# Weight preparation of a seven-product feed-forward kernel: from bf16 on single buffers to byte pairs and fp8 on double buffers

## The chip, the cores and the metric

The kernel runs on all 8 cores of one Trainium2 chip. Each core takes half of one of the 4 sequences and writes its own 4096 tokens of the output; nothing is exchanged between cores. The metric is the device time of the slowest core, in microseconds. Each core has a matrix engine (TensorE, in the rows PE, with its weight loads as PEld), a vector engine (DVE), a scalar engine (ACT), GpSimd (POOL) and a queue engine (SP). Each works through its own list of instructions in order. Transfers are issued from the queues of SP, ACT and POOL and are carried out by 16 DMA engines.

## The reference

```python
x = L0_attn_x                                  # (4, 8192, 1024) f32
xn = layernorm(x)
k, v, q = fft(xn @ Wk.T + bk), fft(xn @ Wv.T + bv), fft(xn @ Wq.T + bq)
queried = cumsum(k * v, axis=1) * conj(q)
attn = real(ifft(queried / (1e-9 + norm(queried)))) / sqrt(1024)
w(kb) = where(kb, +1.0, -1.0)                  # kb: booleans, one byte each
h = s0 * (concat([xn, -xn]) @ w(k0))           # k0 (2048, 4096)
h = s1 * (relu(h) * 2 @ w(k1))                 # k1 (4096, 4096)
h = s2 * (relu(h) * 2 @ w(k2))                 # k2 (4096, 1024)
out = x + attn + h
```

## The kernel before

A core has 4096 tokens, in 8 tiles of 512 (`t` = 0 to 7). The work has four stages.

1. Normalization of the extra half, a Gram matrix, and the fold of the three attention matrices with the Fourier matrix (0 to about 178 us).
2. The carry: the running sum over the tokens ahead of the core's own. PE and DVE alternate over nine steps (`carry_sums`, `products`); ACT takes its result out of PSUM (`evict(CH_CARRY, ...)`), and DVE scales it.
3. The projection loop, eight tiles. For each tile PE makes 24 chunks of 8 matmuls (`project(t, i)`, L684) and, after chunks 17 and 21, two inverse transforms each of the tile before (`inverse`, L739). ACT takes each chunk out of PSUM (`evict_proj`, recorded at L870), each inverse with two passes (`evict_inverse`, L970 and L973), and normalizes the next tile (`normalize`, L844 to L863). Four PSUM banks serve the chunks, so PE may be four chunks ahead of ACT. DVE takes six chunks at a time: `elementwise(t, mb)`, `mb` = 0 to 3 (L1206 to L1235), needs the eviction of chunk 6·mb+5. Once a tile it makes the `statistics` of the tile after the next (L1054 to L1066).
4. The feed-forward part, layers (0, t), (1, t), (2, t). Each matrix product is done with 7 instead of 8 block products ("P1" to "P7", L818 for layers 0 and 1, L796 for layer 2); ACT copies partial results (`snap`, L1007), DVE adds them. The weight operands are fp8 and stream from DRAM (`w0c`, `w1c`, `w2c`) into a ring.

The seven weight operands have to be made first, from boolean bytes. That is the **weight preparation**. It is cut into 48 units (8 for layer 0, 32 for layer 1, 8 for layer 2). A unit is four quarters of 128x1024, one byte per weight. Before, a unit goes like this:

- its bytes are loaded into `raw` (two buffers): by SP for the units of layer 0, two loads each (`load_first`, L461), otherwise by ACT's queue (L878);
- for layer 0 DVE first combines the two loads, in pairs of bytes (`ternary`, L1084);
- ACT turns all 4096 columns into bf16 +1/-1 (or +1/0/-1), with the sign of the layer's scale in it, in two activations of 3072 and 1024 columns (`prepare` of ACT, L896), into `wq`, of which there are two until tile 7 and one from there on;
- DVE makes the sums of quarters with four bf16 `tensor_sub` (`prepare` of DVE, L1093 to L1098): one into `wq` itself, three into `ws`, of which there is one;
- POOL stores four blocks from `wq` (L1383) and three from `ws` (L1385); both stores change bf16 to fp8 on the way.

ACT may not write a `wq` before its last store has landed, and DVE may not write `ws` before the last store of `ws` has landed (`s_ps`).

The order of all this is written out by hand. DVE has, for tile t of 1 to 7, with units u-5 to u-1 of the tile: elementwise 0, u-5, u-4, elementwise 1, u-3, u-2, elementwise 2, statistics, u-1, elementwise 3 (tile 7 has four units). ACT has u-5, u-4, u-3, u-2, u-1 behind chunks 5, 8, 11, 15 and 19. Seven units (`FIRST_UNITS`) fall in the carry stage and tile 0, and the last seven (`SPOTS`) between the evictions of layer (1, 0).

Of the kernel before, what the change touches and what calls it, by code (L numbers as in the profile page):

```python
# [12 lines left out]
BF16 = mybir.dt.bfloat16  # L13
# [13 lines left out]
NST = 8  # L27
# [122 lines left out]
PROD_AT = {"P1": 0, "P7": 1, "P2": 2, "P4": 3, "P3": 4, "P5": 5, "P6": 6}  # L150
# [14 lines left out]

UNITS = ([(0, mh, m) for mh in range(4) for m in range(2)]
# [3 lines left out]
HALF_UNIT = [u for u in range(len(UNITS)) for _ in range(2 if u < 8 else 1)]  # L170
# [5 lines left out]
FIRST_UNITS = 7  # L176
# [36 lines left out]
def build_nc():  # L213
# [40 lines left out]
    s_ps = sem("s_ps")  # L254
# [27 lines left out]
    s_pa = sem("s_pa")  # L282
    s_snap = sem("s_snap")
# [53 lines left out]
    def layout(part, *specs):  # L337

        made, pos = {}, 0
        with ExitStack() as stack:  # L340
            for at, name, shape, dt, size in specs:
# [29 lines left out]
                *[(40 + 2 * i, f"kv{i}", [128, D], BF16, 2) for i in range(2)],  # L371
                (48, "z1", [128, NMB * D], BF16, 8),
# [42 lines left out]
    xt = {p: ld["xt" + p] for p in ("P4", "P5", "P6", "P7")}  # L415
    xn_b, xa, part_b = ld["xn_b"], [ld[f"xa{i}"] for i in range(4)], [ld[f"part{i}"] for i in range(4)]

    wq, ws = [lc["wq0"], lc["wq1"]], lc["ws"]
    xsum, xsum_h = lb["xsum"], lb["xsum_h"]

    def own_block(t):

        return xn_t if t else lb["xn_t0"]

# [1077 lines left out]
```

## Time and profile before

| | us |
|---|---|
| median of 3 runs | 3181.21 (3179.56 to 3186.8) |
| the profiled execution, its own time | 3180.06 |
| its span, core 4 (the slowest) | 3178.3 |
| spans of the 8 cores | 3163.4 to 3178.3 |
| TensorE busy in the span | 2971.2 (93%) |
| DVE, ACT, POOL busy | 1235.5, 839.8, 216.8 |
| carry stage | 178 to 231 |
| projection loop, eight tiles | 231 to 784 |
| feed-forward part | 783 to 3178 |

A row of the timeline has the start, the duration, the engine, the line in the kernel, the operation, output <- input, and how many instructions are merged in it; what stands in brackets is the idle time of the engine ahead of it and what ended it. A row of the waits has who waited for whom, the sum in us, how many times, and the longest. The span starts at 0, and all rows are of core 4.

### The profile page before, as it was taken

To read this page: it belongs to the slowest core of one execution; us is meant where nothing else is said; L and a number is where in the kernel's file an instruction comes from. 1 tells how busy PE (TensorE), PEld (TensorE's weight loads), DVE (VectorE), ACT (ScalarE), POOL (GpSimd) and SP (SyncE) were. 2 spreads that over 40 slices of the span, in tenths; PEclk is the share of its full clock that TensorE was granted. 3 is DMA by queue.
4 is the path that set the end of the run, shared out by engine and by line. 5 is a ranking of instruction groups with operands and counts; after the bars stand their busy time and mean duration, and the time that the engine had idled before them with its cause. 6 is when DMAs were issued, how large, how long until landed. Compare 5 with 4: busy or idle time off the path is not lost.

```text
span 3178.3 us, 57905 instructions; the slowest of 8 cores (3163.4 to 3178.3 us)
## 1 busy us (share of the span) xinstructions
PE 2971.2 (93%) x22472; PEld 2191.4 (69%) x22472; DVE 1235.5 (39%) x2503; ACT 839.8 (26%) x1172; POOL 216.8 (7%) x268
## 2 busy tenths in 40 slices
PE   6787777878999999999999999999999999999997
PEld 3333233334788868868886888688778868886884
DVE  6476566657422522152134124321611251243113
ACT  6345666665331200120111002011200110121000
POOL 7100111111000000000000000000000000000000
PEclk8898898888999999999999999999999999999999
DMA  8675889886687464456446644644564456446543
GB/s 279 186 186 126 178 200 191 198 181 147 187 216 215 157 224 151 136 176 220 152 133 195 203 153 145 234 153 140 169 223 151 132 180 220 150 134 225 161 151 113
DMA packets 235339, 561.68 MB, mean 177 GB/s; under 512 B 54336, under 2 KB 99392, under 8 KB 231488
## 3 DMA queue, kind: packets, MB, share of 16 engines
q1 hardware_dynamic: 166256, 423.21, 43.2%
q0 software_dynamic: 60032, 102.78, 13.8%
q10 hardware_dynamic: 8784, 31.99, 3.4%
q8 instruction: 186, 3.05, 0.4%
q14 instruction: 81, 0.66, 0.1%
HBM read 463.52 MB, written 85.98 MB: 173 GB/s over the span
## 4 chain that ended last, share of the span: by engine, by line
PE 76%; DMA 9%; DVE 8%; issue 3%; SPq 1%; ACT 1%; DVEq 0%; ACTq 0%; POOL 0%; POOLq 0%
PE pd L818 61%; PE pd L796 12%; DMA w1c<-ws 6%; DVE kv L1218 1%; DVE stats L1054 1%; DMA xring<-x_extra 1%; PE pd L684 1%; SPq L481 1%; DMA w0c<-ws 1%; DVE wq L1095 1%; DVE ws L1093 1%; DVE ws L1096 1%; DMA wtmp<-Wmat 1%; PE pd L600 0%; DVE ws L1098 0%
## 5 line engine op out<-in xcount | busy, mean ns | idle before, releaser
L818 PE MATMUL pd<-r0P,ring 128*128 128x256 f16 x14336 | 1568.7, 273 | 7.2 <-ACT snap L1007 7.2
L818 PEld LDWEIGHTS pd<-r0P,ring 128*128 128x128 fp8e4 x14336 | 1403.8, 98 | 172.8 <-issue 8.0
L1007 ACT ACTIVATE snap<-pd 128x512 f32<-128x512 f32 x432 | 257.4, 597 | 1732.6 <-PE pd L818 1456.9
L1337 DVE SCALAR_TENSOR_TENSOR r1P<-pd,snap 128x512 f16<-128x512 f32 x128 | 88.5, 692 | 904.0 <-ACT snap L1007 621.1
L796 PE MATMUL pd<-ring,r1P 128*128 128x512 fp8e4 x1792 | 389.8, 380 | 5.1 <-DVE r1P L1354 5.1
L796 PEld LDWEIGHTS pd<-ring,r1P 128*128 128x128 f16 x1792 | 175.7, 98 | 216.3 <-issue 7.5
L1337 DVE SCALAR_TENSOR_TENSOR b<-pd,snap 128x512 f16<-128x512 f32 x128 | 88.6, 692 | 407.3 <-PE pd L818 407.3
L896 ACT ACTIVATE wq<-raw,s_scales 128x3072 bf16<-128x3072 uint8 x96 | 195.8, 2089 | 192.9 <-DMA w1c<-wq 74.6
L818 PE MATMUL pd<-xtP,ring 128*128 128x256 f16 x2048 | 234.4, 272 | 4.7 <-issue 0.9
L684 PE MATMUL pd<-xn_f,Ak 128*128 128x512 f16 x512 | 147.3, 450 | 83.1 <-ACT proj L870 83.0
L818 PEld LDWEIGHTS pd<-xtP,ring 128*128 128x128 fp8e4 x2048 | 195.9, 98 | 38.0 <-issue 13.4
L818 PE MATMUL pd<-xn_b,ring 128*128 128x256 f16 x1536 | 177.4, 275 | 5.8 <-ACT squares L973 5.8
L684 PEld LDWEIGHTS pd<-xn_f,Ak 128*128 128x128 bf16 x512 | 55.6, 111 | 168.6 <-issue 137.0
L818 PEld LDWEIGHTS pd<-xn_b,ring 128*128 128x128 fp8e4 x1536 | 151.7, 99 | 25.5 <-issue 6.3
L684 PE MATMUL pd<-xn_f,Av 128*128 128x512 f16 x512 | 124.0, 398 | 16.9 <-ACT proj L870 16.9
L684 PE MATMUL pd<-xn_f,Aq 128*128 128x512 f16 x512 | 125.4, 402 | 13.8 <-ACT proj L870 13.8
L870 ACT ACTIVATE proj<-pd,bcol 128x512 bf16<-128x512 f32 x192 | 119.9, 691 | 29.2 <-PE pd L684 29.0
L1337 DVE SCALAR_TENSOR_TENSOR r0P<-pd,snap 128x512 f16<-128x512 f32 x128 | 85.5, 687 | 88.8 <-ACT snap L1007 88.4
L684 PEld LDWEIGHTS pd<-xn_f,Av 128*128 128x128 bf16 x512 | 51.7, 102 | 87.3 <-issue 43.5
L684 PEld LDWEIGHTS pd<-xn_f,Aq 128*128 128x128 bf16 x512 | 52.0, 102 | 82.4 <-issue 35.9
L577 PE MATMUL pd<-xn_x 128*128 128x512 f16 (+3 forms) x384 | 74.4, 361 | 29.9 <-ACT xn_x L863 29.9
L1093 DVE TENSOR_TENSOR ws<-wq 128x1024 bf16<-128x1024 bf16 x48 | 33.0, 689 | 162.7 <-DMA w1c<-ws 121.0
(147 smaller groups left out, 1795.4 us busy)
## 6 DMA issues: line engine op xcount, KB each, us to landing
ring<-w1c SPq DMA_DIRECT2D x448, 512.0 KB, 4.0
ring<-w0c SPq DMA_DIRECT2D x224, 256.0 KB, 2.7
ring<-w2c SPq DMA_DIRECT2D x112, 512.0 KB, 4.9
raw<-kraw ACTq DMA_DIRECT2D x39, 512.0 KB, 6.6
xring<-x_extra SPq DMA_DIRECT2D x32, 512.0 KB, 7.9
w1c<-wq POOLq DMA_DIRECT2D x32, 512.0 KB, 5.5
xa<-x_own POOLq DMA_DIRECT2D x32, 512.0 KB, 12.5
out<-xa POOLq DMA_DIRECT2D x32, 512.0 KB, 8.4
```

What stands on the lines that cost most here:

```text
L481: sync.dma_start(xn_f[t % 2][:, dk * TST:(dk + 1) * TST], xn_dram.ap()[t * TST:(t + 1) * TST, dk * 128:(dk + 1) * 128], transpose=True).th ...
L577: mm = te.matmul(pd[pair][:, at:at + hi - lo], xb[:, i * 128:(i + 1) * 128], xb[:, lo:hi], start=(tb == 0 and at % 512 == 0), stop=(tb == ...
L684: mm = te.matmul(bank, sA[p][:, dk * D + cs.start: dk * D + cs.stop], xn_f[t % 2][:, dk * TST:(dk + 1) * TST], start=(dk == 0), stop=(dk = ...
L796: mm = te.matmul(bank, r1[prod_][:, kt * 256 + q * 128: kt * 256 + (q + 1) * 128], ring[n % RING][:, (kt % 8) * 512:(kt % 8 + 1) * 512], s ...
L818: mm = te.matmul(bank[:, mi * 256:(mi + 1) * 256], ring[n % RING][:, at:at + 128], rhs, start=(opens and kt == 0 and mi == 0), stop=(close ...
L870: sc.activation(dst, src, AF.Identity if kw else AF.Copy, **kw).then_inc(s_ev, 1)
L896: op = sc.activation(wq[BUF[u]][:, lo:hi], raw_t[h % 2][:, lo:hi], AF.Identity, scale=s_scales[:, at:at + 1], bias=s_scales[:, to:to + 1])
L1007: sc.activation(snap[i][q][:], banks[0][q], AF.Copy, scale=scale).then_inc(s_snap, 1)
L1054: own(v.bn_stats(stats[b][:, (2 * j + h) * 6:(2 * j + h + 1) * 6], xring[x_slot(c)][:, h * 512:(h + 1) * 512]))
L1093: own(v.tensor_sub(s1, a21, a22))
L1095: v.tensor_sub(a21, a11, a21).then_inc(s_pq, 1)
L1337: v.scalar_tensor_tensor(dst[q], banks[bk][q], scale, snap[si][q][:], op0=OP.mult, op1=OP.add).then_inc(done, 1)
```

## The change

It replaces the number format and the buffers of the weight preparation and reorders it.

- **Layers 1 and 2, per unit.** DVE writes three quarters as finished fp8 bytes straight from `raw`, two bytes at a time as one uint16 (two `tensor_scalar`, 1024 and 512 elements, into `w8q`). It makes the four sums, again in pairs of bytes (512 elements each), with three `scalar_tensor_tensor` and one `tensor_sub`, into `sums` (uint8). ACT converts `sums` to fp8 `w8s`, in two activations of 3072 and 1024 columns.
- **Layer 0, per unit.** The combination of the two loads goes to its own buffer `tern`. ACT converts three quarters of `tern` to fp8 (2048 and 1024 columns, `prepare_quarters`), and later the sums.
- **Stores** take fp8 as it is: three blocks from `w8q`, four from `w8s`. There are two of `raw`, `w8q`, `sums` and `w8s`, and one of `tern`.
- **Loads of `raw`** are all issued by POOL, in between its stores (`load_raw`).
- **Order.** DVE now comes ahead of ACT in each unit; before it was behind. The places on ACT are the same for tiles 1 to 7. DVE's places move ahead by one elementwise. Eight units are in the carry stage and tile 0, six in layer (1, 0).
- **Signs** of s0 and s1 are no longer in the weights but in the scale that ACT and DVE use when they take products out of PSUM (`layer_scale`).
- The sum "P5" of the normalized input overwrites its place in `xn_b`; the order of blocks in DRAM and of quarters in `kraw` changes.

```diff
-FIRST_UNITS = 7
+FIRST_UNITS = 8
...
-BUF = [u % 2 if u < OWN_UNITS[NST - 1][0] else 0 for u in range(len(UNITS))]
...
+                *[(108 + 4 * i, f"w8s{i}", [128, 4 * 1024], F8, 4) for i in range(2)],
+                (116, "tern", [128, 4 * 1024], U8, 4),
...
+                *[(192 + 4 * i, f"sums{i}", [128, 4 * 1024], U8, 4) for i in range(2)],
+                *[(200 + 3 * i, f"w8q{i}", [128, 3 * 1024], F8, 3) for i in range(2)])
...
+    def layer_scale(layer):
+
+        return (s_scales[:, 8:9], s_scales[:, 4:5], 1.0)[layer]
...
+        def convert(dst, src, scale, bias):
+
+            at = 10 + (-4, -3, -1, 1).index(bias)
+            return sc.activation(dst, src, AF.Identity, scale=scale, bias=s_scales[:, at:at + 1], saturate=False)
+
+        def prepare_quarters(u):
+
+            sc.wait_ge(s_tern, u + 1)
+            if u >= 2:
+                sc.wait_ge(s_po[u % 2], 16 * (u // 2))
+            convert(w8q[u % 2][:, 0:2048], tern[:, 0:2048], 1.0, -1)
+            convert(w8q[u % 2][:, 2048:3072], tern[:, 2048:3072], -1.0, 1).then_inc(s_pa0, 1)
+
         def prepare(u):
...
+            scale = 2.0 if UNITS[u][0] else 1.0
+            sc.wait_ge(s_pd, u + 1)
+            if u >= 2:
+                sc.wait_ge(s_ps[u % 2], 16 * (u // 2))
+            convert(w8s[u % 2][:, 0:3072], sums[u % 2][:, 0:3072], scale, -4)
+            convert(w8s[u % 2][:, 3072:4096], sums[u % 2][:, 3072:4096], scale, -3).then_inc(s_pa, 1)
...
-        for u in range(3):
+        for u in range(4):
+            prepare_quarters(u)
             prepare(u)
         evict(CH_CARRY, red[:], singles[CH_CARRY % 4][:, 0:12])
...
-            if i in (2, 8, 14, 20):
-                prepare(3 + i // 6)
+            if i % 6 == 1:
+                prepare_quarters(4 + i // 6)
+            if i % 6 == 4:
+                prepare(4 + i // 6)
...
+                v.scalar_tensor_tensor(tern[:].bitcast(U16), raw_t[0][:].bitcast(U16), 257.0,
+                                       raw_t[1][:].bitcast(U16), op0=OP.add, op1=OP.subtract).then_inc(s_tern, 1)
...
+                own(v.tensor_scalar(q[:, 0:1024], src[:, 0:1024], -128.0, float(0xB8B8), op0=OP.mult, op1=OP.add))
+                v.wait_ge(s_dve, nv)
+                v.tensor_scalar(q[:, 1024:1536], src[:, 1024:1536], 128.0, float(0x3838),
+                                op0=OP.mult, op1=OP.add).then_inc(s_pq, 1)
...
+            own(v.scalar_tensor_tensor(o1, a21, f * 0x0101, a22, op0=OP.add, op1=OP.add))
+            own(v.scalar_tensor_tensor(o7, a11, f * 0x0202, a21, op0=OP.add, op1=OP.subtract))
             v.wait_ge(s_dve, nv)
...
+            own(v.tensor_sub(o2, o1, a11))
             v.wait_ge(s_dve, nv)
-            v.tensor_sub(s4, a12, s2).then_inc(s_pd, 1)
+            v.scalar_tensor_tensor(o4, a12, f * 0x0303, o2, op0=OP.add, op1=OP.subtract).then_inc(s_pd, 1)
...
         for mb in range(NMB):
+            prepare(4 + mb)
             elementwise(0, mb)
-            prepare(3 + mb)
-            ternary(4 + mb)
         for t in range(1, NST):
             units = list(OWN_UNITS[t])
-            elementwise(t, 0)
             if t < NST - 1:
                 prepare(units[-5])
             prepare(units[-4])
+            elementwise(t, 0)
+            prepare(units[-3])
             elementwise(t, 1)
-            prepare(units[-3])
             prepare(units[-2])
...
+            g.dma_start(dst[:, 0:3], w8q[u % 2][:].rearrange("p (r k) -> p r k", r=3)).then_inc(s_po[u % 2], 16)
+            if layer and u + 2 < len(UNITS):
+                load_raw(u + 2)
+            g.wait_ge(s_pa, u + 1)
+            g.dma_start(dst[:, 3:7], w8s[u % 2][:].rearrange("p (r k) -> p r k", r=4)).then_inc(s_ps[u % 2], 16)
```

The three places where the order of instructions matters for what follows. First DVE in tile 1 to 5, from the statistics (L1054 before) to the start of elementwise 3 (`u<-proj`). Before:

```order
L1054 BN_STATS stats<-xring 128x6 x8
L1058 BN_AGGR mv<-stats 128x2 x4
L1064 TENSOR_SCALAR nmean<-mv 128x4
L1066 COPY var<-mv 128x4
L1093 TENSOR_TENSOR ws<-wq 128x1024
L1095 TENSOR_TENSOR wq<-wq 128x1024
L1096 TENSOR_TENSOR ws<-ws,wq 128x1024
L1098 TENSOR_TENSOR ws<-wq,ws 128x1024
L1206 TENSOR_TENSOR u<-proj 128x1024
```

The same place in the changed kernel:

```order
L1032 BN_STATS stats<-xring 128x6 x8
L1036 BN_AGGR mv<-stats 128x2 x4
L1042 TENSOR_SCALAR nmean<-mv 128x4
L1044 COPY var<-mv 128x4
L1075 TENSOR_SCALAR w8q<-raw 128x1024
L1077 TENSOR_SCALAR w8q<-raw 128x512
L1087 SCALAR_TENSOR_TENSOR sums<-raw 128x512
L1088 SCALAR_TENSOR_TENSOR sums<-raw 128x512
L1090 TENSOR_TENSOR sums<-sums,raw 128x512
L1092 SCALAR_TENSOR_TENSOR sums<-raw,sums 128x512
L1199 TENSOR_TENSOR u<-proj 128x1024
```

The unit stands at the same place, but its input is `raw` and no longer ACT's `wq`: here DVE waited for ACT before, and ACT waits for DVE now.

Second ACT at the end of the carry stage: the units between the normalization of tile 1 and the eviction of the carry (`red<-pd`), and the first of tile 0. Before:

```order
L896 ACTIVATE wq<-raw,s_scales 128x3072
L896 ACTIVATE wq<-raw,s_scales 128x1024
L896 ACTIVATE wq<-raw,s_scales 128x3072
L896 ACTIVATE wq<-raw,s_scales 128x1024
L870 ACTIVATE red<-pd 128x12
L870 ACTIVATE proj<-pd,bcol 128x512 x3
L896 ACTIVATE wq<-raw,s_scales 128x3072
L896 ACTIVATE wq<-raw,s_scales 128x1024
L870 ACTIVATE proj<-pd,bcol 128x512 x6
```

In the changed kernel:

```order
L856 ACTIVATE w8q<-tern,s_scales 128x2048
L856 ACTIVATE w8q<-tern,s_scales 128x1024
L856 ACTIVATE w8s<-sums,s_scales 128x3072
L856 ACTIVATE w8s<-sums,s_scales 128x1024
L851 ACTIVATE red<-pd 128x12
L851 ACTIVATE proj<-pd,bcol 128x512 x2
L856 ACTIVATE w8q<-tern,s_scales 128x2048
L856 ACTIVATE w8q<-tern,s_scales 128x1024
L851 ACTIVATE proj<-pd,bcol 128x512 x3
L856 ACTIVATE w8s<-sums,s_scales 128x3072
L856 ACTIVATE w8s<-sums,s_scales 128x1024
L851 ACTIVATE proj<-pd,bcol 128x512 x3
```

A unit of layer 0 now has two places on ACT instead of one, and the eviction of the carry stands behind four units instead of three.

Third POOL in the projection loop. Before, and then in the changed kernel:

```order
L1383 DMA w1c<-wq 128x4x1024
L1385 DMA w1c<-ws 128x3x1024
L1383 DMA w1c<-wq 128x4x1024
L1385 DMA w1c<-ws 128x3x1024
L1390 DMA partial_dram<-eo 128x1024 x2
```

```order
L1396 DMA w1c<-w8q 128x3x1024
L1382 DMA raw<-kraw 128x4096
L1400 DMA w1c<-w8s 128x4x1024
L1396 DMA w1c<-w8q 128x3x1024
L1382 DMA raw<-kraw 128x4096
L1400 DMA w1c<-w8s 128x4x1024
L1405 DMA partial_dram<-eo 128x1024 x2
```

The load of a unit's bytes has moved in between the two stores of the unit two ahead of it.

## Rows read from the trace of the kernel before

**Rows 1.** The page: busy time, and chain that ended last by line.

```profile
PE 2971.2 (93%) x22472; PEld 2191.4 (69%) x22472; DVE 1235.5 (39%) x2503; ACT 839.8 (26%) x1172; POOL 216.8 (7%) x268
...
PE pd L818 61%; PE pd L796 12%; DMA w1c<-ws 6%; DVE kv L1218 1%; DVE stats L1054 1%; DMA xring<-x_extra 1%; PE pd L684 1%; SPq L481 1%; DMA w0c<-ws 1%; DVE wq L1095 1%; DVE ws L1093 1%; DVE ws L1096 1%; DMA wtmp<-Wmat 1%; PE pd L600 0%; DVE ws L1098 0%
```

**Rows 2.** Waits, 300 to 784 us (DVE and ACT).

```profile
DVE ws L1093 <- DMA w1c<-ws: 121.0, 18, 11.5
DVE ws L1093 <- DMA w0c<-ws: 17.7, 2, 11.8
...
ACT wq L896 <- DMA w1c<-wq: 74.6, 16, 9.9
```

**Rows 3.** Timeline of ACT: evictions that end tile 0 and tile 7.

```profile
298.61 2.39 ACT L870 ACTIVATE proj<-pd,bcol 128x512 bf16<-128x512 f32 x4
...
782.93 1.29 ACT L870 ACTIVATE proj<-pd,bcol 128x512 bf16<-128x512 f32 x2
```

**Rows 4.** Timeline of DVE, 516 to 540 us: statistics, one unit, two elementwise.

```profile
516.01 4.84 DVE L1054 BATCH_NORM_STATS2 stats<-xring 128x6 f32<-128x512 f32 x8
...
521.99 0.69 DVE L1093 TENSOR_TENSOR ws<-wq 128x1024 bf16<-128x1024 bf16 x1
...
524.79 0.69 DVE L1206 TENSOR_TENSOR u<-proj 128x1024 bf16<-128x1024 bf16 x1
...
531.51 0.68 DVE L1206 TENSOR_TENSOR u<-proj 128x1024 bf16<-128x1024 bf16 x1
...
538.92 0.41 DVE L1235 COPY z<-u 1x1024 bf16<-1x1024 bf16 x1
```

**Rows 5.** Timeline of ACT, 572 to 584 us: one unit, evictions, two inverses.

```profile
572.75 4.08 ACT L896 ACTIVATE wq<-raw,s_scales 128x3072 bf16<-128x3072 uint8 x2 [4.09 <-DMA w1c<-wq]
576.74 1.24 ACT L870 ACTIVATE proj<-pd,bcol 128x512 bf16<-128x512 f32 x2
577.88 1.00 ACT L970 CAST eo<-pd 128x1024 bf16<-128x1024 f32 x1
...
581.67 2.45 ACT L870 ACTIVATE proj<-pd,bcol 128x512 bf16<-128x512 f32 x4
```

**Rows 6.** Groups by line and shape, 0 to 1000 us: busy, mean ns.

```profile
L896 ACT ACTIVATE wq<-raw,s_scales 128x3072 bf16<-128x3072 uint8 x48 | 141.6, 2949 | 192.9 <-DMA w1c<-wq 74.6 <-DVE raw L1084 45.1 <-DMA w2c<-wq 42.3
...
L896 ACT ACTIVATE wq<-raw,s_scales 128x1024 bf16<-128x1024 uint8 x48 | 59.0, 1230 | 0.0
...
L1084 DVE SCALAR_TENSOR_TENSOR raw<-raw 128x2048 uint16<-128x2048 uint16 x8 | 18.3, 2288 | 3.3 <-DMA raw<-kraw 3.3
...
L1231 DVE TENSOR_TENSOR z<-y 128x512 bf16<-128x512 bf16 x32 | 13.4, 420 | 0.0
...
L1341 DVE TENSOR_SCALAR r0P<-r0P 128x512 f16<-128x512 f16 x16 | 3.9, 285 | 0.0
...
L1235 DVE COPY z<-u 1x1024 bf16<-1x1024 bf16 x8 | 3.3, 415 | 0.8
```

**Rows 7.** The instructions that touch the tile `raw`, 500 to 585 us: its loads.

```profile
DMA to landing us min/median/max: 5.2/7.1/13.6
```

**Rows 8.** Timeline of ACT, 231 to 259 us: eviction of the carry, a unit of tile 0.

```profile
231.20 0.18 ACT L870 ACTIVATE red<-pd 128x12 f32<-128x12 f32 x1 [9.21 <-PE pd L700]
...
258.66 4.08 ACT L896 ACTIVATE wq<-raw,s_scales 128x3072 bf16<-128x3072 uint8 x2 [7.39 <-DVE raw L1084]
```

**Rows 9.** Timeline of DVE, 227 to 230 us: the ninth and last `products`.

```profile
227.81 1.21 DVE L1172 TENSOR_TENSOR prod<-brow_k,pd 1x1024 bf16<-1x1024 bf16 x1 [5.06 <-PE pd L718]
```

**Rows 10.** Waits of PE, 784 to 3178 us.

```profile
PE pd L818 <- ACT snap L1007: 7.2, 1, 7.2
```

**Rows 11.** Timeline of PE: layer (1, 0) from 847 us, the start of (0, 1), and (1, 1).

```profile
847.22 84.03 PE L818 MATMUL pd<-r0P,ring 128*128 128x256 f16 x768
...
1052.35 3.66 PE L818 MATMUL pd<-xn_b,ring 128*128 128x256 f16 x32
...
1150.84 195.79 PE L818 MATMUL pd<-r0P,ring 128*128 128x256 f16 x1792
```

More of the change, by code:

```diff
@@ L253, in build_nc @@
     s_po = [sem(f"s_po{i}") for i in range(2)]
-    s_ps = sem("s_ps")
+    s_ps = [sem(f"s_ps{i}") for i in range(2)]
     s_xnw = sem("s_xnw")
@@ L414, in build_nc @@
     r1 = {p: ld["r1" + p] for p in ORDER}
-    xt = {p: ld["xt" + p] for p in ("P4", "P5", "P6", "P7")}
+    xt = {p: ld["xt" + p] for p in ("P4", "P6", "P7")}
     xn_b, xa, part_b = ld["xn_b"], [ld[f"xa{i}"] for i in range(4)], [ld[f"part{i}"] for i in range(4)]
-    wq, ws = [lc["wq0"], lc["wq1"]], lc["ws"]
+    tern, sums = lc["tern"], [lc["sums0"], lc["sums1"]]
+    w8q, w8s = [lc["w8q0"], lc["w8q1"]], [lc["w8s0"], lc["w8s1"]]
     xsum, xsum_h = lb["xsum"], lb["xsum_h"]
@@ L994, in _ @@
         for layer, t in LAYERS:
-            scale = C1 if layer == 1 else 1.0
+            scale = layer_scale(layer)
             if (layer, t) == (1, 0):
@@ L1007, in _ @@
                         sc.activation(snap[i][q][:], banks[0][q], AF.Copy, scale=scale).then_inc(s_snap, 1)
-                    for u in SPOTS.get((layer, t, pair, i), ()):
-                        prepare(u)
+                    if (layer, t, pair, i) in SPOTS:
+                        prepare(SPOTS[(layer, t, pair, i)])
                 if layer < 2:
@@ L1016, in _ @@
                                       scale=scale).then_inc(s_c21a, 1)
-                for u in SPOTS.get((layer, t, pair, 3), ()):
-                    prepare(u)
+                if (layer, t, pair, 3) in SPOTS:
+                    prepare(SPOTS[(layer, t, pair, 3)])
                 if (layer, t) == (0, 0):
@@ L1131, in _ @@
         v.wait_ge(s_dve, nv)
-        for dst, src, f in ((4, 7, 2.0), (5, 7, -1.0), (6, 7, -2.0), (9, 8, -1.0)):
-            own(v.tensor_scalar(s_scales[:, dst:dst + 1], s_scales[:, src:src + 1], f, None, op0=OP.mult))
+        own(v.tensor_scalar(s_scales[:, 4:5], s_scales[:, 7:8], C1, None, op0=OP.mult))
         own(v.scalar_tensor_tensor(s_scales[:, 0:1], s_scales[:, 0:1], 2048.0, s_scales[:, 8:9],
@@ L1155, in _ @@
         gram_done(v)
-        own(v.memset(ones_t[:], 1.0))
         own(v.memset(t16[:], TC * GSCALE))
@@ L1280, in _ @@
         for layer, t in LAYERS:
[L1281 removed]
+            scale = layer_scale(layer)
             if (layer, t) == (1, 0):
@@ L1341, in _ @@
                         own(v.tensor_scalar(dst[q], dst[q], 0.0, None, op0=OP.max))
-                    for u in SPOTS.get((layer, t, pair, i), ()):
-                        prepare(u)
+                    if (layer, t, pair, i) in SUM_SPOTS:
+                        prepare(SUM_SPOTS[(layer, t, pair, i)])
                 v.wait_ge(s_dve, nv)
@@ L1355, in _ @@
                                  b21[q]).then_inc(s_r0 if layer == 0 else s_r1, 1)
-                for u in SPOTS.get((layer, t, pair, 3), ()):
-                    prepare(u)
+                if (layer, t, pair, 3) in SUM_SPOTS:
+                    prepare(SUM_SPOTS[(layer, t, pair, 3)])
                 if layer == 1 and pair == 1 and t + 1 < NST:
@@ L1422, in _ @@
                 for i in range(4):
-                    for u in SPOTS.get((layer, t, pair, i), ()):
-                        store_unit(u)
+                    if (layer, t, pair, i) in SPOTS:
+                        store_unit(SPOTS[(layer, t, pair, i)])
             if layer == 0 and t + 1 < NST:
```

152 lines of the change are left out of this document (62 added, 90 removed).

## Prediction, made before the run

> **What bounds the kernel now.** I read the page first, then the chain that ended last, the waits of the engines, and last the timelines of DVE and ACT side by side. By the page PE is busy 93% of the span, and the chain goes through PE's feed-forward lines for 73% of it; the next line is a transfer, `w1c<-ws`, with 6% [rows 1]. So there are two regimes. In the feed-forward part PE is the bound, and nothing in the weight preparation can change that except where PE stands still: once, 7.2 us, for a `snap` of ACT [rows 10]. In layer (1, 0) PE needs 205.1 us (847.22 to 1052.35) for what it does in 195.6 us in layer (1, 1) (195.79, the last matmul overlapping the next): 9.5 us are lost there [rows 11].
>
> The other regime is the projection loop. From the end of tile 0 (298.61 and three evictions of 0.58, the fourth is tile 1's: 300.3) to the end of tile 7 (784.2) it takes 483.9 us for seven tiles, 69 us each [rows 3]. None of the engines is full in it; DVE waits 121.0 and 17.7 us for stores of `ws` to land, ACT 74.6 us for stores of `wq` [rows 2]. With one `ws` a unit can't begin before the store of the last has landed. The change removes just this. The question is what comes late next.
>
> **The cost of a unit after the change.** DVE's prices from rows: a two-source operation on 512 two-byte elements 0.42, the `scalar_tensor_tensor` on 2048 uint16 2.29, so one element per cycle, and 0.69 for 512 (2.29 less 1536 elements at 1.04 ns); one-source operations on two-byte elements in SBUF 0.285 for 512 and 0.415 for 1024 [rows 6]. Two instructions follow each other 0.08 us before the end of the first, or 0.1 us after it where the second waits for it: the old unit, four of 0.69, takes 2.80 so (521.99 to 524.79) [rows 4]. A new unit of layers 1 and 2 is then 0.52 + 0.20 + 0.61 + 0.79 + 0.52 + 0.61 = 3.25 us, and a unit of layer 0 is 2.39 + 2.53 = 4.9. No row has a one-source operation on uint16. Its bounds are the rows above (0.42 and 0.285) and one element per cycle, 1.21 for 1024 (here with an input in PSUM) [rows 9] and 0.69 for 512, which would make the unit 4.45. I take the lower one, since the rows of bf16 and f16 agree with each other and differ from uint16 in the type alone; the upper one is a rival. ACT's unit stays at 4.0 us (572.75 to 576.74) [rows 5], because the same 3072 and 1024 columns go through; fp8 out instead of bf16 has no row, and what speaks for the same price is that ACT's time goes by columns (1230 and 2949 ns for 1024 and 3072) [rows 6]. The quarters of layer 0 come to 2.09 + 1.23 less the overlap of 0.17, 3.15 us.
>
> The Trainium skill ("Vector Engine (DVE) Microarchitecture Reference", section 5.1) asks for two-byte types, and not for floats, before a one-source operation takes four elements per cycle, and does not list `scalar_tensor_tensor` among the operations that have a fast mode. By it the unit is 3.25; no run here shows it for uint16 yet.
>
> **The loop after the change, step by step.** Elementwise is 6.7 us (524.79 to 531.51), 7.75 with row 0 (531.51 to 539.25), statistics 6.0 (516.01 to 521.99) [rows 4], an eviction 0.58, two inverses 3.8 to 3.9 (577.88 to 581.67) [rows 5]. I begin at the last eviction of a tile, which frees elementwise 3:
>
> - DVE: elementwise 3 (6.7), two units (6.5), elementwise 0 (7.75), unit u-3 (3.25), elementwise 1 (6.7), unit u-2 (3.25): 34.15. In this stretch ACT is ahead of DVE except at u-3, where it catches up.
> - ACT at chunk 15 has been waiting for this unit: conversion 4.0, evictions 16 and 17, 1.2: 5.2.
> - DVE, which waited for chunk 17: elementwise 2 (6.7), statistics (6.0), unit u-1 (3.25): 15.95.
> - ACT at chunk 19 has been waiting for that: conversion 4.0, evictions 20 and 21, two inverses, evictions 22 and 23: 10.3.
>
> With four hand-offs of 0.1 that is 66.0 us. The wait for the store is gone, but DVE's unit now stands ahead of ACT's, and ACT's conversions of u-2 and u-1 stand ahead of the evictions that DVE needs. So DVE's idle time of 5.2 and 10.3 us a tile takes the place of the waits for `ws`. PE is hidden: while ACT waits it fills the four banks. The stores are hidden: each has over 14 us until its buffer is wanted, and the same buffer is two units away. Tile 6 has no statistics, 60.0. Tile 7 has one unit fewer too, 56.7; its sums of the input (four operations of 0.69) fit in the 5.2 us in which DVE waits. Tiles 1 to 7: 330 + 60.0 + 56.7 = 446.7, against 483.9: **37.2 us less**.
>
> **The carry stage and tile 0.** Here work is added. The eviction of the carry, at 231.2 now [rows 8], stands behind four units. DVE's last `products` end at 230.3 (227.81 and 2.5) [rows 9]; without the waits for `raw` (3.3 us in all [rows 6]) and with a first unit that is 2.6 us longer I put them at 228.5. Then `tern` (230.8), ACT's quarters (234.1), its sums (238.1), the eviction 238.4. Carry 1.2, statistics 6.0, `tern` 2.4: 248.0; quarters 3.15, three evictions, sums 4.0, one eviction: chunk 5 at 257.6. From there each six chunks take one elementwise, `tern` 2.4, quarters 3.2, four evictions 2.3, sums 4.0 and 0.2 of hand-offs: 19.8, 18.8, 18.8. Tile 0 ends at 315.0, against 300.3: **14.7 us more**. Now the distance of two units is 18.0 (258.66 to 276.64 in the timeline whose first row is in rows 8).
>
> **Layer (1, 0).** Six units instead of seven, each of DVE one step ahead of ACT's, and a store buffer that is two units old. ACT's conversion of 4.0 us stands behind a `snap` and ahead of the next, which PE wants only two products (14 us) later. I find no wait that would reach PE: **9.5 us less**, all of it. The signs in the evictions change an immediate into a scalar operand; costed at nothing, since DVE and ACT wait for PE there. The order of the sums of the input, one longer chain (0.8 us), lies behind layer 1's work of PE.
>
> **Sum.** 14.7 - 37.2 - 9.5 = -32.0. I take 1 off for hand-offs that I haven't seen and get -31: 3180.06 - 31 = 3149, and the median shown is 1.15 above that execution: **3150 us**.
>
> **Rivals.**
>
> *One element per cycle for the uint16 `tensor_scalar`* (the slower side). A unit is 1.2 us longer. All of DVE's units in tiles 1 to 7 are on the path above, 5 x 5 + 5 + 4 = 34: +41 us, so 3150 + 41 = 3191, slower by 0.3%. It decides from 0.9 us a unit on. For it: the uint16 operation that has a row runs so; against it: that one has two sources. 10%.
>
> *Loads of `raw` come late from POOL's queue.* The load of u-3 is issued when DVE is done with u-5, and is wanted after u-4 and elementwise 0, 3.25 + 7.75 = 11.0 us later. A load lands in 5.2 to 13.6 us now, median 7.1 [rows 7]. If all took 13.6 the tile would be 2.6 us longer, 7 x 2.6 = 18: 3168. The other loads have 20 us and more. Against it: stores read half the bytes in SBUF, so the queues are emptier. 8%. The Trainium skill ("SBUF — State Buffer", section "SBUF: two separate sides") has a rule that bears on it: while DVE runs an operation that uses both port pairs, GpSimd can't write descriptors, and it advises the ACT or SP queue. By that each load could be late by one such operation, 0.42 us, inside the slack of 3.9; so far no row here shows such a delay.
>
> *The waits go and nothing replaces them.* If ACT's conversions were not in DVE's way, DVE would lose its 15.5 us a tile, 7 x 15.5 = 108: 3042. For it: the engines are each busy under 50 us a tile. Against it: the lists are in order, and the evictions of chunks 16 and 20 stand behind conversions. 5%.
>
> *The stores stay the bound.* If fp8 stores landed no sooner than 13.8 us and the two buffers did not help, the projection loop would stay and tile 0 would cost its 14.7: 3181 + 14.7 - 9.5 = 3186. Against it is the distance of two units. 3%.
>
> **How the numbers follow.** The forecast has 74%, its own range 3150 +- 14 (2 us a tile); the rivals 10, 8, 5 and 3%. The range from 3130 to 3174 holds the forecast but for a few per cent, and the late loads, about 79%; I widen it to 3128 to 3176. A measurement of this kernel can tell about 0.2%, 6 us. Faster by more than that: forecast, late loads, no replacement, less a tail: 0.84. Within: 0.05. Slower: 0.11.
>
> **What would show it.** In the profile after: DVE's `w8q<-raw` at 0.42 and 0.285 us; no DVE wait for a store in the loop, but DVE waiting for ACT's `proj` twice a tile, about 5 and 10 us, and ACT's `w8s` waiting for DVE's `sums`, up to 11 us; tile 0 ending near 315 and tile 7 near 762; tiles of 66 us; PE without a gap in layer (1, 0). It is wrong if tiles take under 60 or over 70 us, if ACT's conversion is longer than 4.1 us, or if the first tile ends before 305.

## The result, and the profile after

The changed kernel takes **3149.4 us** (median of 20 executions). Against the kernel before on the same chip that is a ratio of **0.9909**, 95% interval 0.9886 to 0.9931, so 22 to 36 us less. In some executions one die or both ran at a lower granted clock and took up to 15% longer, with most of the kernels here; such executions (they lift the median of before to 3207 us) are left out of all that follows. The forecast was 3150 us, in a range from 3128 to 3176.

The profiled execution took 3149.38 us, and the span of its slowest core (core 5) is 3147.8. First come two lines of the page, to be read against [rows 1]: busy time, and the chain that ended last by line.

```profile
PE 2952.8 (94%) x22472; PEld 2187.8 (70%) x22472; DVE 1272.4 (40%) x2579; ACT 898.1 (29%) x1188; POOL 246.6 (8%) x324
...
PE pd L799 62%; PE pd L777 12%; PE pd L665 7%; DVE stats L1032 2%; ACT w8s L856 1%; ACT proj L851 1%; DMA xring<-x_extra 1%; PE pd L720 1%; DVE kv L1211 1%; DVE tern L1066 1%; SPq L472 1%; DMA wtmp<-Wmat 1%; PE pd L581 0%; PE pd L696 0%; DVE wsd L1052 0%
```

The store `w1c<-ws` with its 6% is gone from the chain. Next come the waits of DVE and ACT from 300 to 765 us (total, times, longest), to be read against [rows 2]:

```profile
DVE u L1199 <- ACT proj L851: 114.0, 15, 10.7
...
ACT w8s L856 <- DVE sums L1092: 121.6, 27, 11.7
```

No wait for a store is left in that stretch, and each engine waits for the other. The timeline of DVE for the second half of one tile (start, duration, in brackets the idle time before) shows where, beside the statistics at 491.72:

```profile
476.00 0.42 DVE L1075 TENSOR_SCALAR w8q<-raw 128x1024 uint16<-128x1024 uint16 x1
...
478.66 0.69 DVE L1092 SCALAR_TENSOR_TENSOR sums<-raw,sums 128x512 uint16<-128x512 uint16 x1
485.00 0.69 DVE L1199 TENSOR_TENSOR u<-proj 128x1024 bf16<-128x1024 bf16 x1 [5.64 <-ACT proj L851]
...
500.72 0.69 DVE L1092 SCALAR_TENSOR_TENSOR sums<-raw,sums 128x512 uint16<-128x512 uint16 x1
511.77 0.69 DVE L1199 TENSOR_TENSOR u<-proj 128x1024 bf16<-128x1024 bf16 x1 [10.36 <-ACT proj L851]
```

ACT's timeline beside it: the conversion that had waited for these sums runs first, and of the evictions behind it the two at 483.58 and the first two of the four at 510.30 are what DVE waits for.

```profile
479.78 3.90 ACT L856 ACTIVATE w8s<-sums,s_scales 128x3072 fp8e4<-128x3072 uint8 x2 [4.06 <-DVE sums L1092]
483.58 1.24 ACT L851 ACTIVATE proj<-pd,bcol 128x512 bf16<-128x512 f32 x2
...
501.56 3.89 ACT L856 ACTIVATE w8s<-sums,s_scales 128x3072 fp8e4<-128x3072 uint8 x2 [11.74 <-DVE sums L1092]
505.36 1.24 ACT L851 ACTIVATE proj<-pd,bcol 128x512 bf16<-128x512 f32 x2
...
510.30 2.46 ACT L851 ACTIVATE proj<-pd,bcol 128x512 bf16<-128x512 f32 x4
```

The same timeline has the eviction of the carry and those that end tile 0 and tile 7, to be read against [rows 3, 8]:

```profile
236.75 0.16 ACT L851 ACTIVATE red<-pd 128x12 f32<-128x12 f32 x1
...
311.45 1.26 ACT L851 ACTIVATE proj<-pd,bcol 128x512 bf16<-128x512 f32 x2
...
760.98 1.30 ACT L851 ACTIVATE proj<-pd,bcol 128x512 bf16<-128x512 f32 x2
```

Of the last pair at 311.45 the first ends tile 0, at 312.1; tile 7 ends at 762.3. Tiles 1 to 7 take 450.2 us instead of 483.8. In the feed-forward part PE's timeline shows layer (1, 0) without a gap, but PE's waits from 761 to 3147 us have 31 short waits for `snap`. Before, there was one wait for `snap`, in layer (1, 0) [rows 10]; that its 7.2 us equal the new sum is chance:

```profile
823.19 195.79 PE L799 MATMUL pd<-r0P,ring 128*128 128x256 f16 x1792
```

```profile
PE pd L799 <- ACT snap L985: 7.2, 31, 0.4
```

The groups by line and shape (busy, mean ns) are to be read against [rows 6]:

```profile
L985 ACT ACTIVATE snap<-pd,s_scales 128x512 f32<-128x512 f32 x384 | 263.5, 687 | 1463.8 <-PE pd L799 1462.3 <-DMA partial_dram<-eo 1.5
...
L856 ACT ACTIVATE w8s<-sums,s_scales 128x3072 fp8e4<-128x3072 uint8 x48 | 136.9, 2852 | 121.8 <-DVE sums L1092 121.8
L1331 DVE SCALAR_TENSOR_TENSOR r1P<-pd,s_scales,snap 128x512 f16<-128x512 f32 x128 | 96.1, 751 | 908.1 <-ACT snap L985 627.1 <-PE pd L799 281.0
...
L856 ACT ACTIVATE w8s<-sums,s_scales 128x1024 fp8e4<-128x1024 uint8 x48 | 54.5, 1135 | 0.0
...
L985 ACT ACTIVATE snap<-pd 128x512 f32<-128x512 f32 x48 | 28.7, 597 | 274.3 <-PE pd L777 274.3
...
L1075 DVE TENSOR_SCALAR w8q<-raw 128x1024 uint16<-128x1024 uint16 x40 | 16.7, 418 | 0.4 <-issue 0.4
...
L1077 DVE TENSOR_SCALAR w8q<-raw 128x512 uint16<-128x512 uint16 x40 | 11.8, 295 | 4.2
```

### The profile page after: what moved, and what is told of

The parts are those of the page before. It is cut to its first block, busy times and chain, and to the rows that moved or that the text cites. A ratio compares the mean times of both kernels' runs of the same rounds, so it can differ in the third digit from the quotient of the medians.

```text
span 3147.8 us, 58054 instructions; the slowest of 8 cores (3140.1 to 3147.8 us)
## 1 busy us (share of the span) xinstructions
PE 2952.8 (94%) x22472; PEld 2187.8 (70%) x22472; DVE 1272.4 (40%) x2579; ACT 898.1 (29%) x1188; POOL 246.6 (8%) x324
## 4 chain that ended last, share of the span: by engine, by line
PE 84%; DVE 6%; issue 4%; ACT 3%; DMA 2%; SPq 1%; ACTq 0%; DVEq 0%; POOLq 0%; POOL 0%
PE pd L799 62%; PE pd L777 12%; PE pd L665 7%; DVE stats L1032 2%; ACT w8s L856 1%; ACT proj L851 1%; DMA xring<-x_extra 1%; PE pd L720 1%; DVE kv L1211 1%; DVE tern L1066 1%; SPq L472 1%; DMA wtmp<-Wmat 1%; PE pd L581 0%; PE pd L696 0%; DVE wsd L1052 0%
## 5 line engine op out<-in xcount | busy, mean ns | idle before, releaser
L985 ACT ACTIVATE snap<-pd,s_scales 128x512 f32<-128x512 f32 x384 | 263.5, 687 | 1463.8 <-PE pd L799 1462.3
L1331 DVE SCALAR_TENSOR_TENSOR r1P<-pd,s_scales,snap 128x512 f16<-128x512 f32 x128 | 96.1, 751 | 908.1 <-ACT snap L985 627.1
L1331 DVE SCALAR_TENSOR_TENSOR b<-pd,s_scales,snap 128x512 f16<-128x512 f32 x128 | 96.0, 751 | 395.5 <-PE pd L799 391.8
L799 PE MATMUL pd<-xn_b,ring 128*128 128x256 f16 x2048 | 237.7, 274 | 7.7 <-ACT squares L949 7.7
L799 PEld LDWEIGHTS pd<-xn_b,ring 128*128 128x128 fp8e4 x2048 | 201.3, 98 | 32.8 <-issue 8.1
L856 ACT ACTIVATE w8s<-sums,s_scales 128x3072 fp8e4<-128x3072 uint8 x96 | 186.7, 1994 | 121.8 <-DVE sums L1092 121.8
L799 PE MATMUL pd<-xtP,ring 128*128 128x256 f16 x1536 | 183.4, 272 | 7.3 <-ACT snap L985 7.2
L799 PEld LDWEIGHTS pd<-xtP,ring 128*128 128x128 fp8e4 x1536 | 145.9, 97 | 34.4 <-issue 15.6
L1331 DVE SCALAR_TENSOR_TENSOR r0P<-pd,s_scales,snap 128x512 f16<-128x512 f32 x128 | 93.1, 748 | 82.9 <-PE pd L799 78.9
L985 ACT ACTIVATE snap<-pd 128x512 f32<-128x512 f32 x48 | 28.7, 597 | 274.3 <-PE pd L777 274.3
```

The costliest lines, as they stand in the source:

```text
L799: mm = te.matmul(bank[:, mi * 256:(mi + 1) * 256], ring[n % RING][:, at:at + 128], rhs, start=(opens and kt == 0 and mi == 0), stop=(close ...
L856: return sc.activation(dst, src, AF.Identity, scale=scale, bias=s_scales[:, at:at + 1], saturate=False)
L985: sc.activation(snap[i][q][:], banks[0][q], AF.Copy, scale=scale).then_inc(s_snap, 1)
L1331: v.scalar_tensor_tensor(dst[q], banks[bk][q], scale, snap[si][q][:], op0=OP.mult, op1=OP.add).then_inc(done, 1)
```

## The experiments

The theory: in the changed projection loop DVE and ACT take turns, because ACT's conversions of a tile's fourth and fifth unit wait for DVE's sums and stand ahead of evictions that DVE needs next; the stores are hidden by the second buffers, whatever their bytes. Its rivals: the stores or the loads are what is late; or PE is. All times are read on the slowest core; "tile 0" runs from the eviction of the carry to the last eviction of tile 0, "tiles 1-7" from there to that of tile 7. Ratios are to the kernel before in the same chip's runs, where it took 3178 to 3186 us. The two kernels without a ratio ran on a chip on which the kernel before has a single execution to compare with, and the one with the conversion's scale as a column was itself run once.

```
kernel                          us    ratio (95%)               tile 0  tiles 1-7
before                        3180    1                          69.2    483.8
changed                       3149    0.991 (0.989 to 0.993)     75.4    450.2
fourth unit moved             3122    0.980 (0.978 to 0.982)     75.4    422.0
fifth unit moved              3093    0.971 (0.968 to 0.974)     75.4    394.5
both moved                    3073    0.965 (0.962 to 0.968)     75.4    373.1
all places moved              3068    0.964 (0.962 to 0.967)     64.6    385.6
only carry and tile 0 moved   3131    -                          64.6    450.8
DVE's units as before         3245    1.020 (1.018 to 1.021)     75.4    548.2
changed, one deep             3191    1.003 (1.001 to 1.005)     75.4    493.5
before, two of ws             3116    0.978 (0.976 to 0.980)     68.4    434.6
changed, scale as a number    3145    0.989 (0.987 to 0.990)     75.4    450.2
conversion's scale a column   3153    -                          76.8    451.3
```

### The places of ACT's conversions

```
-            at = dict(zip((19, 15, 11, 8, 5), reversed(OWN_UNITS[t])))
+            at = dict(zip((23, 17, 11, 8, 5), reversed(OWN_UNITS[t])))
```

> The changed kernel with ACT's conversions of the last two units of a tile moved behind the evictions that DVE needs: the fourth unit from chunk 15 to chunk 17, the fifth from chunk 19 to chunk 23. Nothing is added or left out. Theory (in the changed kernel's projection loop DVE and ACT take turns: 5.6 + 10.4 us of a 66 us tile DVE waits for evictions that stand behind a conversion): both waits of DVE go, and a tile falls from 66.4 us to 51 to 55 us; over seven tiles 70 to 95 us less, 3149 becomes 3055 to 3080 us, and the first feed-forward matmul moves from 761 to about 680 us. Rival A (the waits go and something else is just as late: transfers of raw or of the stores, now asked for more often): tiles stay above 60 us, the time above 3110 us. Rival B (PE is what is late, since evictions and conversions both hold banks): tiles of 64 to 66 us, the time within 10 us of 3149 us.

3073 us, a tile 53 us. The waits in the loop (DVE, then ACT, 310 to 682 us) are these:

```profile
DVE u L1199 <- ACT proj L851: 30.5, 20, 8.5
```

```profile
ACT proj L851 <- PE pd L665: 28.0, 34, 1.4
ACT eo L946 <- PE pd L720: 14.7, 14, 1.3
ACT w8s L856 <- DMA w1c<-w8s: 6.2, 3, 2.2
```

DVE's idle time fell from 114 to 30 us, and ACT, which had waited for DVE, now waits for PE. With two numbers changed this kernel is quicker than both the kernel before and the changed one: 3.5% below before, where the change brought 0.9%. The halves, `(23, 15, ...)` and `(19, 17, ...)`:

> The changed kernel with only the conversion of the fifth unit of a tile moved, from chunk 19 to chunk 23. Theory: the 10.4 us in which DVE waits for chunk 23 go, less what ACT's conversion at chunk 23 holds up in the next tile; a tile of about 57 us, 3149 becomes 3080 to 3095 us. Rivals: that wait only moves to the next tile's first units, which need this conversion's buffer two units later: tiles of 66 us, 3149 us; or the transfers take its place: above 3110 us.

> The changed kernel with only the conversion of the fourth unit of a tile moved, from chunk 15 to chunk 17. Theory: the 5.6 us in which DVE waits for chunk 17 go and nothing else does; a tile of about 62 us, 3149 becomes 3115 to 3125 us. Rivals: unchanged, 3149 us, if the wait is for PE and not for the conversion; above 3140 us if the transfers are next.

3093 and 3122 us, both as the theory has it. Tiles 1-7 are 56 and 28 us shorter, a little more in sum than the 77 of both moved.

### Two buffers alone, and the change without them

In the kernel before, a second `ws` in two pieces (at 116 and 44 KB):

```
+            if SBUF[u]:
+                s4, s1, s2 = ws1b[:], ws1a[:, 0:D], ws1a[:, D:2 * D]
...
-                v.wait_ge(s_ps, 16 * u)
+            sums_stored(v, u, (SBUF[u],))
```

> The kernel before with one thing of the change alone: a second buffer for the sums ws (bf16, as it was), used from the fourth unit to the last of tile 6. One of the two is in two pieces, so its store is two transfers. The arithmetic, the order of the work, ACT's conversions before DVE's sums, seven first units and seven units in layer (1, 0) are those of the kernel before. Theory (the store's latency behind a single buffer set the tiles of before, and in the change's order ACT and DVE wait for each other instead): DVE's 17 us a tile of waits for stores go and nothing replaces them, since before's ACT converts ahead of DVE's need; tiles of 69 us fall to 55 to 60 us, 3178 becomes 3100 to 3125 us, faster than the changed kernel. Rival (the gain of the change is its fewer stored bytes or its cheaper arithmetic): tiles stay at 65 us or more, 3150 to 3178 us.

3116 us: the second buffer alone brings 2.2%, over twice what the whole change does. The tiles of 62 us are longer than the 55 to 60 expected. The waits from 300 to 733 us (DVE's two longest, then ACT's) say why:

```profile
DVE u L1217 <- ACT proj L879: 38.1, 9, 7.1
DVE ws L1104 <- ACT wq L905: 37.8, 11, 9.6
```

```profile
ACT wq L905 <- DMA w1c<-wq: 51.2, 13, 7.6
ACT proj L879 <- PE pd L693: 29.6, 27, 3.6
ACT wq L905 <- DMA raw<-kraw: 20.6, 5, 8.1
```

With `ws` out of the way the store of `wq` and the load of `raw` are next. In the changed kernel neither shows, and with both conversions moved, at tiles of 53 us, only 6.2 us of waits for a store do (above). So something else in the change helps as well; whether it is the fewer bytes or the order of loads and stores, no run separates. The other way round, the changed kernel with a wait for the unit just before:

```
                 v.wait_ge(s_po[i], 16 * (u // 2))
+                v.wait_ge(s_po[1 - i], 16 * ((u + 1) // 2))
...
+            if u > FIRST_UNITS:
+                sc.wait_ge(s_ps[1 - u % 2], 16 * ((u + 1) // 2))
```

> The changed kernel with the second buffer made useless from the ninth unit on: DVE's quarters of a unit and ACT's conversion of its sums wait until the stores of the unit just before have landed, as one buffer would have it. Arithmetic, bytes and order are unchanged. Theory (two buffers are what hides the stores): DVE and ACT wait for stores again, tiles of 75 to 80 us, 3149 becomes 3205 to 3235 us. Rival (the fewer bytes of fp8 alone make the stores quick enough): tiles of 66.5 us, 3149 us.

3191 us, not 3205 to 3235: I had priced the stores too high. But the rival falls, since without its second buffers the change makes the kernel 0.3% slower than before. Waits for stores are back, 87 us in all where the kernel before had 213 [rows 2], beside the turns that the two engines take (ACT, then DVE, 311 to 804 us):

```profile
ACT w8s L856 <- DVE sums L1095: 107.8, 21, 11.5
ACT w8s L856 <- DMA w1c<-w8s: 53.6, 12, 6.9
```

```profile
DVE w8q L1078 <- DMA w1c<-w8q: 33.8, 6, 7.3
```

### DVE's order

```
-            if t < NST - 1:
-                prepare(units[-5])
-            prepare(units[-4])
             elementwise(t, 0)
-            prepare(units[-3])
+            if t < NST - 1:
+                prepare(units[-5])
+            prepare(units[-4])
             elementwise(t, 1)
+            prepare(units[-3])
             prepare(units[-2])
```

> The changed kernel with DVE's units in the places of the kernel before: elementwise 0, units one and two, elementwise 1, units three and four, elementwise 2, instead of units one and two, elementwise 0, unit three, elementwise 1, unit four, elementwise 2. ACT's places are those of the changed kernel. Theory (what sets a tile is how often DVE and ACT hand over to each other, since now DVE's sums come before ACT's conversion): ACT's conversions wait for units that stand behind an elementwise, and that elementwise for evictions behind the conversion; a tile of 75 to 82 us, 3149 becomes 3210 to 3250 us. Rival (only the store or the two places found so far hold DVE): 64 to 68 us a tile, 3135 to 3160 us.

3245 us, tiles of 80.9 us. DVE now waits four times a tile (28 times from 310 to 857 us) instead of two:

```profile
DVE u L1199 <- ACT proj L851: 201.0, 28, 10.7
```

The order that suited conversions ahead of the sums costs 95 us when they come behind.

### The carry stage and tile 0

```
         for u in range(4):
+            if u == 3:
+                evict(CH_CARRY, red[:], singles[CH_CARRY % 4][:, 0:12])
             prepare_quarters(u)
...
-            if i % 6 == 4:
+            if i % 6 == 5:
                 prepare(4 + i // 6)
```

Together with the places of tiles 1 to 7, and then alone:

> The changed kernel with every place moved at which ACT's conversion stands ahead of an eviction that DVE needs next: in tiles 1 to 7 the fourth unit from chunk 15 to 17 and the fifth from 19 to 23 (which alone gave 3074 us), in tile 0 the conversion of the sums from the fifth to behind the sixth chunk of each six, and the eviction of the carry ahead of the fourth unit instead of behind it. Nothing is left out. Theory: in tile 0 elementwise no longer waits for the 4.0 us conversion, four times, and tile 0 after the carry falls from 75.3 us to 60 to 65 us; the carry leaves ACT 5 to 9 us sooner, of which DVE, which is busy with the fourth unit, passes on about 4. Tile 0 ends 14 to 20 us sooner than in the changed kernel, tiles 1 to 7 take 365 to 373 us as in the run with both conversions moved, and the time is 3050 to 3062 us. Rival (tile 0 is held by tern and quarters alone, or by PE): tile 0 after the carry stays at 73 to 76 us, and the time at 3068 to 3075 us.

> The changed kernel with only the two moves in the carry stage and tile 0: the eviction of the carry ahead of the fourth unit, and in tile 0 the conversion of the sums behind the sixth chunk of each six instead of the fifth. Tiles 1 to 7 are those of the changed kernel. Together with the moves in tiles 1 to 7 they made tile 0 end 19 us sooner but the whole only some 6 us shorter. Theory (there the 13 us were lost because in tiles 1 to 7 PE had become the bound, and on one die ran at a lower granted clock; where DVE and ACT set the tiles, what tile 0 gains stays): tile 0 ends 19 us sooner against the last statistics, tiles 1 to 7 take 450 to 453 us, 3149 becomes 3128 to 3134 us. Rival (tile 1 gives the gain back in every arrangement, since its chunks wait for something of its own such as the input's transposes): tile 1 takes 70 us or more, and the time is 3140 to 3149 us.

Tile 0 did what was expected: it took 64.6 us and ended 19 us sooner, counted from DVE's first `tern`. Alone the two moves brought 18 us (3131), as expected. With all places moved they brought nothing that the intervals could tell (0.964 beside 0.965), and the time, 3068 us, missed the 3050 to 3062 expected: tiles 1 to 7 took 385.6 us, not 365 to 373. The table by stretch (core, window, busy time of PE, PEld, DVE, ACT, POOL, granted clock, DMA share, GB/s) compares a core of either die in the execution with all places moved, over a stretch in which both are in the projection loop:

```profile
core 0 of [0, 1, 2, 3, 4, 5, 6, 7], span 3063.3 us
...
310.00:650.00 340.00, 332.25 (x1376) 142.30 (x1375) 284.46 (x585) 283.73 (x333) 78.19 (x118) 0.89 0.82 235
```

```profile
core 4 of [0, 1, 2, 3, 4, 5, 6, 7], span 3036.7 us
...
310.00:650.00 340.00, 324.82 (x1457) 144.88 (x1470) 300.26 (x614) 297.80 (x355) 81.30 (x123) 0.98 0.88 241
```

On core 0 PE is busy 98% of the stretch at a mean granted clock of 0.89 of the upper level of 2.4 GHz, and runs 1376 matmuls; on core 4 it is busy 96% at 0.98 and runs 1457. Tiles 1 to 7 take 383 to 386 us on the first die and 364 to 367 on the second. So on the first die PE is now the bound of the projection loop, and its clock sets the time.

The mean hides two kinds of lower clock. Of these 340 us core 0 spent 190 at a granted 0.81 and 3 at 0.50, the lower level of 1.2 GHz; core 4 spent 22 and 7. In the changed kernel the same stretch has a mean of about 0.9 too, but its cores spent 51 to 68 us at 0.50 and 0 to 49 at 0.81. Why one die had more of the 0.81 than the other is not shown. How full PE is need not be all of it: in the run with only carry and tile 0 moved, on another chip and with PE still pausing (busy 82 to 86% of 310 to 670 us), the cores spent 81 to 152 us at 0.81.

### The scalar operand

```
-        return (s_scales[:, 8:9], s_scales[:, 4:5], 1.0)[layer]
+        return (1.0, C1, 1.0)[layer]
```

> The changed kernel with the scale of the evictions in the feed-forward part given as a number instead of a column of s_scales, as in the kernel before. The signs of the first two layers' scales are left out of the computation by it; nothing else is. Theory (the scalar operand makes ACT's snap 0.09 us and DVE's scalar_tensor_tensor 0.06 us longer, and PE waits for them at the start of a pair in layer 0): snap 597 ns and not 687, the tiles of layer 0 take 50.1 us and not 50.5, PE's 7 us of waits for snap in layer 0 are gone, and with the ends of layers 1 and 2 the feed-forward part is 3 to 4 us shorter: 3145 to 3147 us. Rival (the waits come from the other order of the input's sums or of the stored products): tiles of layer 0 stay at 50.5 us.

3145 us. The 4 us less than the changed kernel would not be clear by the intervals (0.987 to 0.990 beside 0.989 to 0.993); the trace decides. The groups, and what is left of PE's waits from 762 to 3145 us:

```profile
L985 ACT ACTIVATE snap<-pd 128x512 f32<-128x512 f32 x432 | 257.9, 598 | 1771.8 <-PE pd L799 1494.3 <-PE pd L777 274.8 <-DMA partial_dram<-eo 2.7
L1331 DVE SCALAR_TENSOR_TENSOR r1P<-pd,snap 128x512 f16<-128x512 f32 x128 | 88.5, 692 | 911.2 <-ACT snap L985 628.0 <-PE pd L799 283.2
```

```profile
PE pd L799 <- ACT squares L949: 7.7, 1, 7.7
PE pd L777 <- DVE r1P L1348: 5.4, 1, 5.4
```

No wait for `snap` is left, and the tiles of layer 0 take 50.1 us instead of 50.5. In the other direction, a column for the conversions (`scale=s_scales[:, by:by + 1]`, with `by` 13, 12 or 9 for 1, -1, 2):

> The changed kernel with the scale of ACT's conversions to fp8 read from a column of s_scales (1, -1 or 2, as before a value for each partition) instead of given as a number. The result is the same. In the changed kernel the two conversions of the sums took 2852 and 1135 ns, against 2949 and 1230 ns for as many columns to bf16 in the kernel before, where the scale was a column. Theory (the 96 ns are the price of the column, as in the evictions, and fp8 out costs what bf16 out did): 2945 to 2950 and 1225 to 1235 ns, and 0.4 us a tile more. Rival (fp8 out is quicker to write than bf16): 2852 and 1135 ns as they are.

```profile
L857 ACT ACTIVATE w8s<-sums,s_scales 128x3072 fp8e4<-128x3072 uint8 x48 | 141.3, 2943 | 115.8 <-DVE sums L1094 115.8
...
L857 ACT ACTIVATE w8s<-sums,s_scales 128x1024 fp8e4<-128x1024 uint8 x48 | 58.9, 1228 | 0.0
```

2943 and 1228 ns, where bf16 out took 2949 and 1230 [rows 6]: fp8 out costs what bf16 out did. Tiles 1 to 7 took 451.3 us, 0.2 us a tile more and not the 0.4 expected.

## Where the prediction was right, and where it failed

In the projection loop the mechanism held: the waits for the store went, and two waits of DVE for ACT took their place. The step that failed is the one on the signs in the evictions, "costed at nothing, since DVE and ACT wait for PE there": the runs show PE waiting for ACT's `snap` 31 times in layer 0, which costs about 3 us. Two terms were mis-sized: the carry stage and tile 0, forecast at +14.7 us, measured +10.1, and the loop, forecast at -37.2, measured -33.7. That the sum came out to within 1 us is luck in part, since these misses have both signs and cancel. Forecast were -32.0 us and 1 of reserve; the two spans differ by 30.5.

- **The unit of DVE.** It takes 3.35 us from 476.00 to the end of the operation at 478.66; less the overlap of 0.08 that is 3.27, forecast 3.25. The uint16 operations took 418 and 295 ns, the price of the lower bound, so the first rival falls. The Trainium skill ("Vector Engine (DVE) Microarchitecture Reference", section 5.1), by which two-byte types and not floats are what counts, agrees.
- **The unit of ACT** was costed at 4.0 us and took 3.8. I had the type changed and the columns kept, and overlooked that the scale had become a number: 0.1 us less for each of the two instructions.
- **The loop.** Forecast were waits of DVE of 5.2 and 10.3 us and tiles of 66.0, 60.0 and 56.7; measured 5.64 and 10.36, and 66.5 (mean of five), 60.2 and 57.5. The gain was 33.7 and not 37.2 us. The term at fault is the hand-off, taken as 0.1 us each. In the rows above they are 0.43 (479.35 to 479.78), 0.18 (484.82 to 485.00), 0.15 and 0.24: 1.0 a tile, 0.6 more, of which the shorter conversions gave back 0.4. The rest, 0.3 a tile, I did not assign.
- **The carry stage and tile 0** were forecast at +14.7 us. DVE's first `tern` starts at 182.04 now and at 180.50 before, so counted from it the carry came 4.0 us later (54.7 against 50.7), not 7.2, and tile 0 took 6.1 us more, not 7.5: +10.1. What was mis-sized most is the end of the `products`: the last starts at 225.09, 43.0 us after the first `tern`, where I had 45.5. It is also a number in which the core matters: from `tern` to carry the cores of before took 47.0 to 50.7 us, all of the changed kernel 54.7.
- **Layer (1, 0)** lost its 9.5 us on the slowest core (205.1 to 195.6), as forecast. But the layer took 196.2 to 205.6 us on the eight cores of before, in the middle 199.4, so over half of this term belongs to two or three cores and not to the layer; the span of the median core fell by 25.5 us, not 30.5. Which part of the change took the gap away stays open. With two `ws` alone it was there still on most cores (195.6 to 202.0), but that kernel is back to a single `ws` in this layer, so it says little. With the changed kernel one deep the gap was gone (195.6 on all), so it isn't the second buffers by themselves; the seventh unit, the place of ACT's wait for `wq`, the order of the two engines and the fewer bytes are left.
- **The signs in the evictions, costed at nothing**, are the step that was wrong in kind. I wrote that DVE and ACT wait for PE there. That is true in sum (1462 us of ACT's idle time) and false 31 times at the start of a pair in layer 0, where PE waits for `snap`. The column costs ACT 90 ns (597 to 687) and DVE 59 (692 to 751). The last seven tiles of layer 0 are 2.0 us longer together than before, and 2.6 us longer than with the scale as a number. The ends of layers 1 and 2 are longer than before by 0.4 and 0.6, which makes 3.0 us in all. The 0.4 is not the column's, since it stays with the scale as a number (201.2 us against 200.9 before); its cause is open. With the scale as a number the whole feed-forward part is 3.1 us shorter on the slowest core (2383.3 against 2386.4) and 3.0 on the median core. The Trainium skill ("ScalarE: Activation LUTs", section "What ACT_TABLE_LOAD costs") has a price of some 93 ns for each such operand of an ACTIVATE, and these rows agree with it; it would have given the price of both this step and ACT's unit.
- **The sum as measured**: 1.5 (a later start of this stage, in work that the change leaves alone) + 4.0 + 6.1 - 33.7 - 8.6 = -30.7. The -8.6 are PE's part from layer 0 on: -9.5 for layer (1, 0), -2.1 for the first tile of layer 0, +3.0 for its other tiles and the ends of layers 1 and 2.
- **The other rivals.** Loads of `raw` land in 5.9 us (median), and DVE has no wait for them from 300 to 765 us. The port rule of the Trainium skill ("SBUF — State Buffer", section "SBUF: two separate sides") could not be seen in the changed kernel: nothing waited for these loads. That the waits go and nothing replaces them was given 5% and 3042 us; the 15.5 us a tile on which it rested were 16.0, and moving both places gave back 77 us of the 108, until PE is nearly full. That PE stands still only once in the feed-forward part was read too shortly from [rows 10]: it also waited 5.1 us for `r1P` in the last layer and 2.3 us for `squares`, in both kernels nearly alike (5.5 and 2.3 after), so the sum doesn't change. That the stores stay the bound fell, and one deep showed what they cost when not hidden.

## What to carry to other kernels

Where a producer's and a consumer's order is turned round (ACT before DVE, then DVE before ACT), write both in-order lists side by side and look for work that waits for the other engine and stands ahead of what that engine needs: here two places cost 77 us, more than twice what the change brought, and two at the start another 18. Try the second buffer by itself before the rest: here it held more than the whole change. And an operand that is no longer a constant has a price on the engine, which counts even on engines that idle most of the time, if the bound engine waits for single instructions of theirs.

## What the runs showed of the hardware

- A scale read from a column instead of a number costs ACT 90 ns on 512 columns (597 to 687) and 91 to 93 on 3072 and 1024 (2852 to 2943, 1135 to 1228), and DVE's `scalar_tensor_tensor` 59 ns (692 to 751).
- ACT writes fp8 at the price of bf16, in equal form: 2943 and 2949 ns for 3072 columns.
- One die of a chip can run a nearly full PE at a mean granted clock of 0.89 and the other at 0.98 in the same execution, with the same program; tiles 1 to 7 then differ by 19 us between the dies. In the changed kernel, where PE had gaps in this stretch, they took 450.0 to 450.4 us on all cores, though of the 340 us from 310 to 650 they spent 0 to 49 at a granted 0.81.
- The same mean of 0.9 stood for two things: 190 of 340 us at 0.81 with PE 98% busy, and 51 to 68 us at 0.50 with PE some 80% busy.
